# A four-layer graph network on one Trainium2 core: the first pass multiplies the adjacency by h itself, turned, and the weights are applied to its result

## The chip, the core and the metric

The kernel runs on one core of a Trainium2 chip. The core has an engine for matrix products (TensorE; PE in the rows, its weight loads are PEld), VectorE (DVE), ScalarE (ACT), GpSimd (POOL), and a queue (SP) whose only work here is to issue transfers. Each engine runs its own instructions in order and waits on semaphores for the others. The metric is the device time of one execution in microseconds (us); lower is better.

## What is computed

Node features x are 4096 x 256, the adjacency adj is 4096 x 4096. Four layers follow each other, each on h = relu(layernorm(x)). This change touches the first layer only:

```
    def _L0_gnn_ref(X, A, W):
        A2 = A + jnp.eye(A.shape[0], dtype=A.dtype)
        dscale = jnp.diagonal(A2) ** (-0.5)
        temp = A2 @ X @ W.T
        A_norm = dscale[:, None] * A2 * dscale[None, :]
        return jax.nn.relu(A_norm @ temp)
...
    h = jnp.maximum(_layernorm(x, axis=-1), 0.0)
    x = x + _L0_gnn_ref(h, adj, L0_gnn_W)
```

The first layer has two products with the adjacency: `A2 @ (h W^T)`, and then `A_norm @ temp`. The other layers are attention (layer 1), a normalised adjacency (layer 2) and two adjacency products (layer 3).

## The kernel before, in words

The adjacency is read in 8 row groups `g` of 512 rows, and each of these in 8 chunks `c` of 512 columns: 64 chunks of 1 MB per pass. There are six passes `p`: 0 and 1 are the two products of the first layer, 2 is attention, 3 to 5 are the later layers. A step numbered `PRE` ahead of pass 0 makes the moving operand of pass 0.

Every float32 operand of a product is split into two float16 parts, hi and lo, and a product is three matmuls: hi by hi, hi by lo, lo by hi. The hi part of a chunk is made by ScalarE (line L1257 in `split`), the lo part by VectorE (L1650). In pass 0 the split chunk lies in one of 4 `sets`; ScalarE may begin chunk n when TensorE is through with chunk n-4 and the stores of chunk n-4 (its halves, written back to memory for later passes) have landed. From group 1 on VectorE makes two more sums of every chunk (L1657, L1659).

The order on each engine is written out by hand. In `PRE`, for each group q of 512 rows of x: VectorE takes the statistics (`norm_stats`, L1850 to L1858), GpSimd raises the variance to the power -0.5 (L872) and makes the shift (L875), ScalarE writes relu's hi part (L1408), VectorE normalises (L1865) and writes the lo part (L1882), TensorE turns h (L1013), ScalarE copies it (L1417), TensorE multiplies it by the weight (`small`, L1076 to L1078, 24 matmuls) and ScalarE and VectorE split the result (L1445, L1906) into `mov[0]`, which is `right` in the rows. The chunks of group 0 run between these: chunk c needs the rows of x of group c alone. Ahead of them TensorE runs 60 and 60 small matmuls on the identity (`keep_warm`, L1202).

In pass 0 and in attention a block of the adjacency is stationary and 258, 256 and 258 columns of `mov` move past it (L931 to L933): 48 matmuls for a chunk. One of the 258 is a column of ones, which gives the sums of the adjacency's rows. In pass 1 (`CROSS`) the hi block meets hi and lo of `mov[1]` in one matmul of 512 columns (L928), the lo block meets hi in 256 (L929): 32 matmuls for a chunk, and VectorE adds the two halves of the result (`add_cross`, L1742). After each group its tail runs among the chunks of the next: ScalarE takes the accumulators out of PSUM (L1356 in pass 0) behind the split of chunk 0, and so on (`PLACES`).

Of the kernel before, what the change touches and what calls it, by code (L numbers as in the profile page):

```python
# [41 lines left out]
F = 256  # L42
# [20 lines left out]
WARM = [60, 60]  # L63
# [16 lines left out]
def build(nc, x, adj_t, w0, wg, bias_g, w2, bias_2, w3a, w3b, sent, sums, ready, x_mid, directs, out):  # L80
# [4 lines left out]
    with ctx:  # L85
# [6 lines left out]
        def sem(name):  # L92
# [24 lines left out]
        wraw = [shared[:, wofs[i]:wofs[i + 1]].rearrange("p (f n) -> p f n", f=FB) for i in range(5)]  # L117
# [3 lines left out]
        weights_of = {PRE: wpart[0], 1: wpart[1], 2: wpart[2], 3: wpart[3], 4: wpart[4]}  # L121
# [28 lines left out]
        hsp2 = ev[:, :, :].rearrange("p b n -> p (b n)")[:, 0:GB * F].bitcast(f16)\  # L150
            .rearrange("p (b s n) -> p b s n", s=2, b=GB)
# [23 lines left out]
        ident32 = sb("ident32", [P, P], f32)  # L175
        diag = sb("diag", [P, NB], f32)
        d = sb("d", [P, NB], f32)
        dinv = sb("dinv", [P, NB], f32)
# [27 lines left out]
        w0_loaded = sem("w0_loaded")  # L206
# [11 lines left out]
        ones_ready = sem("ones_ready")  # L218
        w_hi = sem("w_hi")
# [86 lines left out]
        SMALL = [PRE, 1, 2, 3, 4]  # L306
        SELF = [0, 1]
# [12 lines left out]
        CROSS = [1]  # L320
        PLAIN = [0, 1]

        def chunk_no(p, g, c):
            return (g + NG * PLAIN.index(p)) * NC + c

# [24 lines left out]
        def whole_of(p, c, k, b):  # L350

            first = k * GR + b * P if p == ATT else block_at(k, b)
            if p == 1 and k >= GB // 2:
                first -= 2 * QUAD
                return halved[c % 4][:, first:first + P], halved[c % 4][:, 2 * QUAD + first:2 * QUAD + first + P]
            hi, lo = sets[c % 4] if p == 0 else sets[c % 2]
            return hi[:, first:first + P], lo[:, first:first + P]

        def used_no(p, g, c):

            return chunk_no(p, g, c) - NC

        def raw_free(eng, p, g, c):

            if p == 0 and isinstance(g, int) and g == 0:
                eng.wait_ge(split_ready, c + 1)
# [7 lines left out]
        def turned_at(p, g):  # L374

            return 2 * NG if p == ATT else 2 * NG + 2 + 2 * g
# [92 lines left out]
        def work(p, g):  # L469

            return (o2, hsp2, 1) if p == PRE and g % 2 else (o, hsp, 0)

        def small_bank(p, b):
# [3 lines left out]
            if p == PRE:  # L477
                bank = (psW[:, :], psS[:, 1, :])[b // 2]
            elif p == 3:
# [11 lines left out]
        def _(sp):  # L491
# [4 lines left out]
            def load(g, c):  # L496
                if not (isinstance(g, int) and g == 0 and c < 4):

                    h, e = (g, c - 4) if c >= 4 else (g - 1, c + 4)
                    raw_free(sp, 0, h, e)  # L500
                row = g * (NC * P) + c * P
                sp.dma_start(ring[c % 4], adj_t[bass.ds(row, P), :]).then_inc(adj_loaded[c % 4], 16)

            def store_whole(g, c):

                rows = ready[bass.ds(g * (NC * P) + c * P, P), :]
                raw_free(sp, 0, g, c)
                hi, lo = sets[c % 4]
                sp.dma_start(rows[:, 0:2 * QUAD], hi[:, 2 * QUAD:4 * QUAD]).then_inc(halves_stored[c % 4], 16)
                sp.dma_start(rows[:, 2 * QUAD:4 * QUAD], lo[:, 2 * QUAD:4 * QUAD]).then_inc(halves_stored[c % 4], 16)  # L510
# [13 lines left out]
            def load_halves(g, c):  # L524

                if isinstance(g, int) and g == 0:
                    sp.wait_ge(halves_stored[c % 4], 32 * (c // 4 + 1))
# [114 lines left out]
            def load_others():  # L642
                for src, dst in zip([wg, w2, w3a, w3b], wraw[1:]):
                    sp.dma_start(dst, src).then_inc(w_loaded, 16)
                with nc.allow_non_contiguous_dma(reason="the diagonal's elements lie apart"):

                    row = GB * GR
                    for r in range(GB):
                        src = bass.AP(adj_t.tensor, block_at(r, r), [[row + 1, P], [(NC + 1) * P * row, NG]])
                        sp.dma_start(diag[:, :].rearrange("p (q r) -> p q r", r=GB)[:, :, r], src)\  # L650
                            .then_inc(diag_loaded, 16)
# [22 lines left out]

            def group_0(g):
                for c in range(2 if isinstance(g, int) and g == 0 else 0, NC):
                    load(g, c)
                    if isinstance(g, int) and g == 0 and c < 4:
                        if c == 3:
                            load_others()  # L680
                        continue
# [76 lines left out]
            sp.wait_ge(x_loaded[0], 16)  # L758
            load_x(1)
            load(0, 0)  # L760
            load_x(2)
            load_x(3)
            load(0, 1)
            for q in range(4, NG):
                load_x(q)
# [33 lines left out]
            for p in range(6):  # L799
# [22 lines left out]
                elif p == 0:  # L822
                    group_0(0)
                    group_0(1)
                    with sp.Fori(2, NG) as g:
                        group_0(g)
# [32 lines left out]
        def _(pool):  # L859
# [18 lines left out]
            def tail(p, g):  # L878
                if p in SELF:
# [3 lines left out]
                    if not (isinstance(g, int) and p == 0):  # L883
# [6 lines left out]
                if p == 0:  # L890
                    pool.wait_ge(row_ready, at([0], p, g, 2, 2))
# [16 lines left out]
            for p in [0, 1, 2, 3]:  # L908
                if p == 0:
                    tail(0, 0)  # L910
                    with pool.Fori(1, NG) as g:
                        tail(p, g)
                else:
                    with pool.Fori(0, NG) as g:
                        tail(p, g)
# [3 lines left out]
        def _(pe):  # L919
            def product(p, g, c, b, k, first, last):  # L920
# [5 lines left out]
                if p in CROSS:  # L926
# [1284 lines left out]
```

## Time and profile before

| | |
|---|---|
| median of 3 runs | 2350.82 us (2348.93 to 2351.11) |
| the profiled execution | 2350.55 us |
| its span, first to last instruction | 2348.8 us |
| before and behind the span | 1.75 us |
| PE busy | 2308.0 us (98%) |
| DVE, ACT, POOL busy | 73%, 48%, 6% |
| mean granted TensorE clock | 0.998 |

The span is the time from the first to the last instruction of the core. Busy is the time in which an engine executes; a matmul's end is modelled, so TensorE's pace is read from the distance between the starts of matmuls. The idle time before an instruction is put down to what released it.

### The profile page before, as it was taken

How to read it: one execution, taken by the hardware profiler on the slowest of the kernel's cores; microseconds unless marked ns; L12 is line 12 of the kernel's file. 1: busy time of each engine (PE TensorE's matmuls, PEld its weight loads, DVE VectorE, ACT ScalarE, POOL GpSimd, SP SyncE). 2: the span in 40 equal slices, each digit the busy share in tenths (PEclk: the TensorE clock that was granted, in tenths of full speed). 3: DMA queues.
4: the chain of work that ended last, by engine and by line, in shares of the span. 5: the costliest groups of instructions: out<-in, count | busy, mean ns of one | idle time of the engine just before them, and what ended most of it. 6: DMA issues, size and time to landing. Idle time of an engine off the chain costs nothing. (4 is left out here: it accounts for less than half of the span.)

```text
span 2348.8 us, 62852 instructions
## 1 busy us (share of the span) xinstructions
PE 2308.0 (98%) x24536; PEld 1936.3 (82%) x24536; DVE 1718.9 (73%) x2765; ACT 1131.4 (48%) x1821; POOL 140.4 (6%) x114
## 2 busy tenths in 40 slices
PE   7999999999999999999999999999999999999999
PEld 6888887666666677777778799999988888899998
DVE  7877867677777777678878967676776766667665
ACT  6634443445544555555545545545554444433332
POOL 2211101101100000000000000000000000000000
PEclk9999999999999999999999999999999999999999
DMA  8699998889887988989999999899898898999997
GB/s 287 223 361 335 355 361 298 254 263 283 274 262 226 263 282 281 280 259 308 320 294 314 298 354 328 302 340 334 302 335 328 316 350 309 329 348 382 373 378 290
DMA packets 291738, 726.86 MB, mean 309 GB/s; under 512 B 76704, under 2 KB 109728, under 8 KB 258848
## 3 DMA queue, kind: packets, MB, share of 16 engines
q1 hardware_dynamic: 291328, 724.42, 89.2%
q8 instruction: 79, 1.29, 0.2%
q10 hardware_dynamic: 288, 0.79, 0.1%
q14 instruction: 43, 0.35, 0.0%
HBM read 574.64 MB, written 138.41 MB: 304 GB/s over the span
## 5 line engine op out<-in xcount | busy, mean ns | idle before, releaser
L931 PE MATMUL acc<-right,ahi 128*128 128x258 f16 x1536 | 419.8, 273 | 4.9 <-DVE o L1742 2.1
L933 PE MATMUL acc<-right,alo 128*128 128x258 f16 x1536 | 419.3, 273 | 0.0
L932 PE MATMUL acc<-right,ahi 128*128 128x256 f16 x1536 | 418.7, 273 | 0.0
L953 PE MATMUL acc<-left,ahi 128*128 128x128 f16 x1536 | 272.0, 220 | 3.7 <-DVE alo L1726 3.7
L957 PE MATMUL acc<-left,alo 128*128 128x128 f16 x1536 | 272.1, 220 | 0.0
L956 PE MATMUL acc<-left,ahi 128*128 128x128 f16 x1536 | 272.0, 220 | 0.0
L1580 ACT ACTIVATE ahi<-en 128x512 f16<-128x512 f32 x256 | 160.3, 626 | 91.2 <-DVE en L2066 88.3
L931 PEld LDWEIGHTS acc<-right,ahi 128*128 128x128 f16 x1536 | 150.2, 98 | 41.2 <-DVE alo L2081 9.8
L928 PE MATMUL acc<-left,ahi 128*128 128x512 f16 x512 | 180.2, 379 | 0.0
L928 PE MATMUL acc<-left,en 128*128 128x512 f16 x512 | 180.2, 379 | 0.0
L953 PE MATMUL acc<-left,adj 128*128 128x128 f16 x1024 | 179.0, 220 | 0.0
L956 PE MATMUL acc<-left,adj 128*128 128x128 f16 x1024 | 178.9, 220 | 0.0
L957 PE MATMUL acc<-left,adj 128*128 128x128 f16 x1024 | 178.9, 220 | 0.0
L957 PE MATMUL acc<-left,en 128*128 128x128 f16 x1024 | 178.1, 219 | 0.0
L953 PE MATMUL acc<-left,en 128*128 128x128 f16 x1024 | 178.1, 219 | 0.0
L956 PE MATMUL acc<-left,en 128*128 128x128 f16 x1024 | 178.1, 219 | 0.0
L2081 DVE SCALAR_TENSOR_TENSOR alo<-en,ahi 128x512 f16<-128x512 f32 x256 | 175.4, 685 | 2.3 <-ACT ahi L1580 2.1
L932 PEld LDWEIGHTS acc<-right,ahi 128*128 128x128 f16 x1536 | 150.3, 98 | 29.9
L933 PEld LDWEIGHTS acc<-right,alo 128*128 128x128 f16 x1536 | 150.3, 98 | 18.7
L953 PEld LDWEIGHTS acc<-left,ahi 128*128 128x128 f16 x1536 | 150.8, 98 | 4.1 <-DVE alo L1726 4.0
L957 PEld LDWEIGHTS acc<-left,alo 128*128 128x128 f16 x1536 | 150.9, 98 | 0.0
L956 PEld LDWEIGHTS acc<-left,ahi 128*128 128x128 f16 x1536 | 150.8, 98 | 0.0
(255 smaller groups left out, 6546.1 us busy)
## 6 DMA issues: line engine op xcount, KB each, us to landing
adj<-in_adj_t SPq DMA_DIRECT2D x192, 512.0 KB, 6.1
adj<-ready SPq DMA_DIRECT2D x96, 1024.0 KB, 7.7
en<-ready SPq DMA_DIRECT2D x96, 1024.0 KB, 7.7
adj<-in_adj_t SPq DMA_DIRECT2D x32, 1024.0 KB, 8.3
en<-in_adj_t SPq DMA_DIRECT2D x32, 1024.0 KB, 8.8
en<-ready SPq DMA_DIRECT2D x64, 512.0 KB, 5.4
en<-sent SPq DMA_DIRECT2D x46, 512.0 KB, 6.9
sent<-en SPq DMA_DIRECT2D x90, 256.0 KB, 4.3
```

What stands on the lines that cost most here:

```text
L928: nc.tensor.matmul(acc[:, b, :].rearrange("p (s n) -> p s n", s=2), hi, both, start=first, stop=False)
L931: nc.tensor.matmul(acc[:, b, 0:n], hi, m[:, jb, 0:n], start=first, stop=False)
L932: nc.tensor.matmul(acc[:, b, 0:F], hi, m[:, jb, LO:LO + F], start=False, stop=False)
L933: return nc.tensor.matmul(acc[:, b, 0:n], lo, m[:, jb, 0:n], start=False, stop=last)
L953: nc.tensor.matmul(to, hi[:, rows], bhi[:, cols], start=first and i % 2 == 0 and b == 0 and k == 0, stop=False, skip_group_check=True)
L956: nc.tensor.matmul(to, hi[:, rows], blo[:, cols], start=False, stop=False, skip_group_check=True)
L957: last = nc.tensor.matmul(to, lo[:, rows], bhi[:, cols], start=False, stop=False, skip_group_check=True)
L1580: nc.scalar.activation(ahi[:, (j // GB) % 2, j % GB * GR:(j % GB + 1) * GR], nums[:, n % NUMS, :], ACT.Copy, scale=P_SCALE).then_inc(num_h ...
L2081: nc.vector.scalar_tensor_tensor(alo[:, (j // GB) % 2, cols], nums[:, n % NUMS, :], P_SCALE, ahi[:, (j // GB) % 2, cols], ALU.mult, ALU.su ...
```

## The change

- `PRE` no longer turns h nor multiplies it by the weight: `first_rows` (ScalarE, L1471 and L1474 of the new file) writes relu's hi part straight to `mov[0]`, and for every group but the first the normalised rows in float32 too, which VectorE wrote before; `lo_of_first_rows` (VectorE) writes the lo part.
- In pass 0 (`first_pass`) a 128 x 128 block of h is stationary and 512 rows of the adjacency move past it: 24 matmuls of 512 columns for a chunk. The result is (A h) turned, in two of the four banks of `acc`; the other two serve the next group. The identity of A2 is added by 16 matmuls for a group (`own_rows`).
- Groups 0 and 1 run in turn (`PAIRED`): chunks (0,0), (1,0), (0,1), (1,1), ... Chunk n of this order is number n. Chunks of group 1 carry VectorE's two sums.
- The tail of a group of pass 0 is two steps: `z` splits the turned result out of PSUM at chunk 0 of the next group, and `t`, at chunk 3, splits what `small` (24 matmuls, behind chunk 2) makes of it with the weight.
- Pass 1 takes the form of pass 0 before: 258, 256 and 258 columns, 48 matmuls for a chunk. The row sums and their power move there, `add_cross` goes.
- 40 matmuls of `keep_warm` instead of 60 and 60. The first chunk is loaded and split in two halves, and the SP queue starts without waiting for x. Weights, biases and the diagonal are loaded between the chunks of the pairs.

```diff
+PAIRED = 2
+            if p == 0 and isinstance(g, int) and g < PAIRED:
+                return PAIRED * c + g
...
+            def turned_block(g, n, c, k, f):
+                hi, lo = moving_of(n, k)
+                rows = mov[0][:, GB * c + k, :]
+                bhi, blo = rows[:, f * P:(f + 1) * P], rows[:, LO + f * P:LO + (f + 1) * P]
+                to = acc[:, 2 * (g % 2) + f, :]
+                nc.tensor.matmul(to, bhi, hi, start=c == 0 and k == 0, stop=False, skip_group_check=True)
+                nc.tensor.matmul(to, bhi, lo, start=False, stop=False, skip_group_check=True)
+                return nc.tensor.matmul(to, blo, hi, start=False, stop=False, skip_group_check=True)
...
+            def first_pass():
+                for n in range(NG * NC):
+                    g, c = place_of(n)
...
+                        pe.wait_ge(split_ready, n + 1)
+                    if g == 0:
+                        pe.wait_ge(mov_ready, at(MOVE, PRE, c, GB, 1 if c == 0 else GB))
+                    if c == NC - 1:
...
+                        own_rows(g)
...
+                    if g >= PAIRED and c == 2:
...
+                        step("W0W1", 0, g - 1 if g > PAIRED else 0)
...
-                if p in CROSS:
-                    both = m[:, jb, :].rearrange("p (s n) -> p s n", s=2)[:, :, 0:F]
-                    nc.tensor.matmul(acc[:, b, :].rearrange("p (s n) -> p s n", s=2), hi, both, start=first, stop=False)
-                    return nc.tensor.matmul(acc[:, b, 0:F], lo, m[:, jb, 0:F], start=False, stop=last)
...
+            def hi_of_z(g, side):
...
+                for f in range(FB):
+                    act.wait_ge(acc_ready, at(ALL, 0, g, GB, 2 * f + 2))
+                    nc.scalar.activation(hTq[:, f, :, :], acc[:, 2 * side + f, :].rearrange("p (b n) -> p b n", n=P),
+                                         ACT.Copy, scale=1.0 / ADJ_SCALE).then_inc(h_hi, GB // FB)
+            def hi_of_t(g):
...
+                for r in range(2):
+                    act.wait_ge(small_ready, at(SMALL, 0, g, 2, r + 1))
+                    for b in (2 * r, 2 * r + 1):
+                        nc.scalar.activation(mov[1][:, blocks(g, b), 0:F], small_out(0, b), ACT.Copy,
+                                             scale=d_w[:, blocks(g, b)]).then_inc(mov_hi, 1)
+            def first_rows(g):
+                act.wait_ge(shift_ready, at(NORM, PRE, g))
...
+                for b in range(GB):
+                    args = dict(bias=shift[:, u, b:b + 1], scale=rstd[:, u, b:b + 1])
+                    nc.scalar.activation(mov[0][:, blocks(g, b), 0:F], xres[:, GB * g + b, :], ACT.Relu, **args)\
+                        .then_inc(mov_hi, 1)
+                    if g > 0:
+                        nc.scalar.activation(normed_of(g)[:, b, :], xres[:, GB * g + b, :], ACT.Identity, **args)\
+                            .then_inc(normed, 1)
...
             split(0, 0, 0)
+            first_rows(0)
             for q in range(NG):
-                keep_hT(q, 0)
-                keep_hT(q, 1)
-                stage("W0", PRE, q)
+                if q > 0:
+                    split(0, 0, q)
+                if q + 1 < NG and q > 0:
+                    first_rows(q + 1)
+                split(0, 1, q)
                 if q == 0:
...
+                    first_rows(1)
...
+            stage("stats", PRE, 0)
+            split_first(0, first_split, first_hi)
+            stage("norm", PRE, 0)
+            lo_of_first_rows(0)
+            split_first(1, split_ready, split_hi)
             stage("stats", PRE, 1)
-            split(0, 0, 0)
             for q in range(NG):
+                if q > 0:
+                    split(0, 0, q)
+                    if q + 1 < NG:
+                        lo_of_first_rows(q + 1)
+                split(0, 1, q)
                 if q == 0:
...
+                    lo_of_first_rows(1)
                 if q + 2 < NG:
                     stage("stats", PRE, q + 2)
```

How this moves instructions is shown at two places. The first is VectorE at the start of the program, one turn of the loop over q. Before, a turn holds one chunk's lo part (L1650), the statistics of group q+2 (L1850 to L1858), and the normalised rows, their lo part and the two halves of the weight's product (L1865, L1882, L1906):

```order
L1850 BN_STATS stats<-left 128x6 x4
L1855 BN_AGGR mv<-stats 128x2 x4
L1857 TENSOR_SCALAR nmean<-mv 128x4
L1858 TENSOR_SCALAR vare<-mv 128x4
L1650 SCALAR_TENSOR_TENSOR right<-en,right 128x2048
L1865 TENSOR_SCALAR en<-left,mv,rstd 128x256 x4
L1906 SCALAR_TENSOR_TENSOR right<-psW,right 128x256 x2
L1882 SCALAR_TENSOR_TENSOR ev<-en,ev 128x4x256
L1906 SCALAR_TENSOR_TENSOR right<-psS,right 128x256 x2
```

Now the same turn reads (L2007 to L2015 are the statistics, L1770 a chunk's lo part, L1896 the lo part of h's rows, L1777 and L1779 the two sums):

```order
L2007 BN_STATS stats<-left 128x6 x4
L2012 BN_AGGR mv<-stats 128x2 x4
L2014 TENSOR_SCALAR nmean<-mv 128x4
L2015 TENSOR_SCALAR vare<-mv 128x4
L1770 SCALAR_TENSOR_TENSOR alo<-adj,ahi 128x2048
L1896 SCALAR_TENSOR_TENSOR right<-en,right 128x4x256
L1770 SCALAR_TENSOR_TENSOR alo<-adj,ahi 128x2048
L1777 TENSOR_TENSOR right<-adj 128x512
L1779 TENSOR_TENSOR right<-right,adj 128x512
```

A second chunk's lo part and its two sums have come in, between the lo part of h's rows and the next statistics; normalising and the weight's product have gone.

The second place is ScalarE in the same turn. Before, it copies the turned h (L1417), takes out the weight's product (L1445), writes relu's four hi parts (L1408) and splits one chunk (L1257):

```order
L1417 ACTIVATE hT<-psT 128x1024
L1417 ACTIVATE hT<-psS 128x1024
L1445 ACTIVATE right<-psW 128x256 x2
L1408 ACTIVATE hsp<-left,shift,rstd 128x256 x4
L1445 ACTIVATE right<-psS 128x256 x2
L1257 ACTIVATE right<-en 128x2048
```

Now it splits a chunk of group 0 (L1345), writes four hi parts (L1471) and four normalised blocks (L1474), and splits the chunk of group 1:

```order
L1345 ACTIVATE right<-en 128x2048
L1471 ACTIVATE right<-left,shift,rstd 128x256
L1474 ACTIVATE o<-left,shift,rstd 128x256
L1471 ACTIVATE right<-left,shift,rstd 128x256
L1474 ACTIVATE o<-left,shift,rstd 128x256
L1471 ACTIVATE right<-left,shift,rstd 128x256
L1474 ACTIVATE o<-left,shift,rstd 128x256
L1471 ACTIVATE right<-left,shift,rstd 128x256
L1474 ACTIVATE o<-left,shift,rstd 128x256
L1345 ACTIVATE right<-en 128x2048
```

The split of the group 1 chunk has come to stand behind eight activations, where it was one chunk a turn behind four.

## Rows read from the trace of the kernel before

**Rows 1.** Page, busy time of each engine and share of the span

```profile
PE 2308.0 (98%) x24536; PEld 1936.3 (82%) x24536; DVE 1718.9 (73%) x2765; ACT 1131.4 (48%) x1821; POOL 140.4 (6%) x114
```

**Rows 2.** Windows: busy of PE, PEld, DVE, ACT, POOL; PEclk, DMA share, GB/s

```profile
21.90:94.00 72.10, 67.00 (x654) 58.99 (x651) 57.57 (x127) 50.08 (x77) 20.21 (x13) 1.00 0.70 218
94.00:390.20 296.20, 294.88 (x2688) 262.74 (x2686) 231.46 (x232) 125.78 (x112) 42.34 (x16) 1.00 0.96 346
390.20:741.40 351.20, 351.20 (x2219) 216.88 (x2217) 250.55 (x444) 166.81 (x328) 43.55 (x37) 1.00 0.84 262
```

**Rows 3.** Waits of PE, 0 to 95 us (total, times, longest)

```profile
PE acc L1202 <- DVE vare L1858: 6.8, 1, 6.8
PE psT L1013 <- DVE ev L1882: 3.7, 4, 1.4
```

**Rows 4.** Timeline of DVE, the start and 20 to 27 us

```profile
4.41 1.41 DVE L1850 BATCH_NORM_STATS2 stats<-left 128x6 f32<-128x256 f32 x4 [3.26 <-DMA left<-in_x]
...
19.73 1.23 DVE L1882 SCALAR_TENSOR_TENSOR ev<-en,ev 128x1024 f16<-128x1024 f32 x1 [0.32 <-ACT ev L1408]
20.87 1.40 DVE L1850 BATCH_NORM_STATS2 stats<-left 128x6 f32<-128x256 f32 x4
...
22.98 2.28 DVE L1650 SCALAR_TENSOR_TENSOR alo<-adj,ahi 128x2048 f16<-128x2048 f32 x1
26.16 1.38 DVE L1865 TENSOR_SCALAR o<-left,mv,rstd 128x256 f32<-128x256 f32 x4 [0.90 <-POOL rstd L872]
```

**Rows 5.** Timeline of POOL, 20 to 35 us

```profile
23.15 2.98 POOL L872 TENSOR_TENSOR rstd<-vare,neghalf 128x4 f32<-128x4 f32 x1 [5.64 <-DVE vare L1858]
...
32.71 1.01 POOL L872 TENSOR_TENSOR rstd<-vare,neghalf 128x4 f32<-128x4 f32 x1 [6.30 <-DVE vare L1858]
```

**Rows 6.** Timeline of ACT, 26 to 29 us

```profile
26.44 2.08 ACT L1408 ACTIVATE hsp<-left,shift,rstd 128x256 f16<-128x256 f32 x4 [1.04 <-POOL shift L875]
28.42 0.63 ACT L1445 ACTIVATE right<-psS 128x256 f16<-128x256 f32 x2
```

**Rows 7.** Timeline of ACT at two group boundaries

```profile
179.84 0.39 ACT L1356 ACTIVATE ev<-acc 128x257 f32<-128x257 f32 x1 [0.93 <-PE acc L933]
180.13 1.90 ACT L1257 ACTIVATE ahi<-adj 128x2048 f16<-128x2048 f32 x1
...
221.98 0.39 ACT L1356 ACTIVATE ev<-acc 128x257 f32<-128x257 f32 x1 [0.93 <-PE acc L933]
```

**Rows 8.** Timeline of DVE behind the first of these boundaries

```profile
182.06 2.29 DVE L1650 SCALAR_TENSOR_TENSOR alo<-adj,ahi 128x2048 f16<-128x2048 f32 x1 [8.93 <-ACT ahi L1257]
...
185.60 1.22 DVE L1807 TENSOR_TENSOR o<-ev,own 128x1024 f32<-128x1024 f32 x1
```

**Rows 9.** Timeline of PE: `small` and behind it, then the end of pass 1

```profile
13.84 0.28 PE L1076 MATMUL psW<-wsp,hT 128*128 128x256 f16 x1 [0.67 <-ACT hT L1417]
...
16.47 3.51 PE L1202 MATMUL acc<-ident 128*128 128x128 f16 x60
...
741.45 0.38 PE L1171 MATMUL psS<-right 128*128 128x512 f16 x1
...
741.88 0.38 PE L1173 MATMUL psS<-right 128*128 128x512 f16 x1
```

**Rows 10.** Waits of PE, 700 us to the end

```profile
PE acc L953 <- DVE alo L1726: 3.7, 1, 3.7
PE acc L931 <- DVE o L1742: 2.1, 1, 2.1
```

**Rows 11.** Windows behind the first of these waits, and early

```profile
1352.00:1354.00 2.00, 2.00 (x20) 2.00 (x21) 0.00 (x0) 0.00 (x0) 0.00 (x0) 0.50 0.97 405
1356.00:1360.00 4.00, 4.00 (x59) 4.00 (x57) 0.00 (x0) 0.26 (x1) 0.00 (x0) 0.76 1.00 412
...
6.00:24.00 18.00, 15.06 (x196) 14.09 (x197) 14.73 (x43) 13.55 (x19) 5.26 (x5) 1.00 1.01 412
```

**Rows 12.** Groups of ACT in pass 1, 440 to 740 us

```profile
L1405 ACT ACTIVATE o<-left,shift,rstd 128x256 f32 x28 | 14.4, 586 | 0.0
```

More of the change, by code:

```diff
@@ L62 @@
 OWN = 5
-WARM = [60, 60]
+WARM = 40
+PAIRED = 2
 LEAD = 3
@@ L467, in sent_rows, with normed_of @@
             return 2 * P * (sum(NC - 1 - h for h in range(g)) + c - g - 1)
-        def work(p, g):
-            return (o2, hsp2, 1) if p == PRE and g % 2 else (o, hsp, 0)
+        def normed_of(g):
+            return (o, o2)[g % 2]
         def small_bank(p, b):
@@ new lines, in own_rows @@
+            def own_rows(g):
+                for f in range(FB):
+                    for b in range(GB):
+                        rows = mov[0][:, GB * g + b, :]
+                        to = acc[:, 2 * (g % 2) + f, b * P:(b + 1) * P]
+                        nc.tensor.matmul(to, rows[:, f * P:(f + 1) * P], scaled_ident[:, :], start=False, stop=False,
+                                         skip_group_check=True)
+                        nc.tensor.matmul(to, rows[:, LO + f * P:LO + (f + 1) * P], scaled_ident[:, :], start=False, stop=False,
+                                         skip_group_check=True)
@@ L1207, in _ @@
             pe.wait_ge(var_ready, 2)
-            keep_warm(WARM[0])
-            pe.wait_ge(w_ready, 1)
-            pe.wait_ge(ones_ready, 1)
-            for s in ["T0T1", "W0", "W1"]:
-                step(s, PRE, 0)
-            keep_warm(WARM[1])
-            step("T0T1", PRE, 1)
+            keep_warm(WARM)
             for p in range(6):
@@ L1256, in split @@
                             act.wait_ge(chunk_done, at(PLAIN, p, g, NC - 1, c - 3 if c >= 4 else c - 2))
-                    nc.scalar.activation(sets[c % 4][0], ring[c % 4], ACT.Copy, scale=ADJ_SCALE).then_inc(split_hi, 1)
+                    if first and c == 0:
+                        act.wait_ge(first_loaded, 16)
+                        for i, made in enumerate((first_hi, split_hi)):
+                            part = slice(i * 2 * QUAD, (i + 1) * 2 * QUAD)
+                            nc.scalar.activation(sets[0][0][:, part], ring[0][:, part], ACT.Copy, scale=ADJ_SCALE).then_inc(made, 1)
+                        return
+                    nc.scalar.activation(sets[n % 4][0], ring[n % 4], ACT.Copy, scale=ADJ_SCALE).then_inc(split_hi, 1)
                     return
+                act.wait_ge(adj_loaded[c % 4], at(PLAIN, p, g, 16 * NC // 4, (c // 4 + 1) * 16))
                 if c >= 2:
@@ L1847, in norm_stats @@
                 dve.sem_inc(passed, 1)
-                u = work(p, g)[2]
+                u = g % 2 if p == PRE else 0
                 for b in range(GB):
@@ L1954, in stage @@
             def stage(name, p, g):
-                if name == "ev" and p in CROSS:
-                    for b in range(GB):
-                        add_cross(p, g, b)
-                elif name == "ev" and p in STR:
+                if name == "ev" and p in STR:
                     mix(p, g)
@@ L2109, in lo_of_weights @@
                 dve.wait_ge(w_hi, n)
[L2110 removed]
+                nc.vector.scalar_tensor_tensor(wsp[:, 1, part], wplain[:, part], W_SCALE, wsp[:, 0, part],
                                                ALU.mult, ALU.subtract).then_inc(w_ready, 1)
[L2114 to L2116 removed]
+            dve.wait_ge(const_ready, 3)
```

471 lines of the change are left out of this document (275 added, 196 removed).

## The prediction, made before the changed kernel ran

> **What bounds the kernel now.** I read the page first: TensorE is busy for 98% of the span and VectorE for 73% [rows 1], so what TensorE does not stream or wait for is worth nothing here. Then windows by stage [rows 2]: in groups 1 to 7 of pass 0 TensorE is busy for 294.9 of 296.2 us, in pass 1 for all 351.2 us. In the stretch with `PRE` and group 0 it is busy for 67.0 of 72.1 us. The waits of the start [rows 3] show where it stands: 6.8 us for the first statistics, and 3.7 us in four waits for h's lo part. So the start is the one place where TensorE already hangs on a chain of the other engines, and the rest is its own stream.
>
> The transfers are near their limit in pass 0 (346 GB/s at a share of 0.96), but 412 GB/s were moved early on [rows 11].
>
> **The change, part by part.**
>
> *Paces.* In pass 0 a group takes 221.98 - 179.84 = 42.1 us [rows 7], or 5.27 us for a chunk of 48 matmuls, 0.110 us each. `small` runs from 13.84 to 16.47: 2.63 us for 24 [rows 9]. A matmul of 512 columns starts 0.215 us behind the last: 741.45 to 741.88 for two [rows 9]. A chunk of 24 of those is 5.17 us. Columns streamed are nearly the same (512 x 24 against 772 x 16), so the new form by itself saves 0.1 us per chunk and no more.
>
> *The rest of pass 0, groups 2 to 7.* 48 chunks x 5.17 = 248.4 us. `own_rows` is 16 matmuls of 128 columns for a group; 60 took 3.51 us [rows 9], so 0.9 us, 5.4 in six groups. `small` stands here seven times: 18.4 us. Sum 272.2 us.
>
> The tails could add to it. `z` needs the group's last matmul. The 257 columns of L1356 take 0.39 us and the next split starts 0.29 us behind their start [rows 7]; two of 512 columns are some 1.2 us, of which half lies under the last matmuls. The split then takes 1.93 us until VectorE starts (180.13 to 182.06) and VectorE 2.29 [rows 7, 8]: 4.9 to 5.0 us behind the group's end, and TensorE wants that chunk at 5.2. `t` waits for `small` behind chunk 2; after it ScalarE has two products' halves, a split, and VectorE a lo part: about 5.1 us behind the end of `small` (0.1 + 0.9 + 1.9 + 2.2), against 5.2 of work. Both just fit; I put 0.1 us for a boundary, 0.7 us in all. If they miss, it is 0.5 us a time, 6 us.
>
> *The start.* This is where the sum is decided. Groups 0 and 1 run in turn, so a group of h's rows feeds two chunks, 10.35 us of work for TensorE. But the engines run in written order, and the order makes a loop: VectorE's statistics of group q+2; GpSimd's power and shift; ScalarE's eight activations of that group; ScalarE's split of chunk (1, q+1), which stands behind them; VectorE's lo part of it and its two sums; then the statistics of q+3. Nothing in that loop overlaps with itself:
> - From the statistics' start to the first activation: 26.44 - 20.87 = 5.57 us [rows 4, 6]. In this the power takes 2.98 us though it takes 1.01 when VectorE stands still [rows 5]: VectorE runs the next chunk's lo part (22.98, 2.28 us) [rows 4], and the power ends 0.87 us behind it. In the new order the same instruction stands behind the statistics, so the same 5.57.
> - Eight activations: four take 28.42 - 26.44 = 1.98 us [rows 6]; 3.96.
> - The split up to VectorE's start: 1.93 [rows 7, 8].
> - The lo part and the two sums: 185.60 - 182.06 = 3.54 [rows 8].
>
> Sum 15.0 us for a pair against 10.35 us of matmuls: TensorE stands for 4.65 us in every pair. Before, a turn held one chunk, turning and `small`; eight of them took 72.1 us with TensorE busy for 67.0 [rows 2], so 9.0 us for 8.4 of work: the waits were small because the loop was short.
>
> Now the clock time. x's first rows land at 4.41 [rows 4]; now 1 MB of the adjacency shares the way, at 412 GB/s up to 2.5 us, and I take 0.8: 5.2. Statistics 2.1, then half a lo part (1.2) and the power's 0.9: 9.5, ScalarE at 9.8. VectorE: normalising 1.38 [rows 4], four lo parts of 0.42, half a lo part 1.2: the statistics of group 1 start near 13.8. TensorE starts at 11.4, where `small` started at 13.8 and pass 0 at 21.9. 13.8 + 5.57 + 3.96 + 1.23 (lo part of the rows, as L1882 [rows 4]) = 24.6: statistics of group 2. Five turns of 15.0 later, at 99.6, those of group 7. From there 5.57 + 3.96 + 1.93 + 2.25 = 13.7: chunk 13 is ready at 113.3. Three chunks (15.5) and two `own_rows` (1.8): 130.6 us, where 16 chunks without a wait would be done at 11.4 + 82.8 + 1.8 = 96.0.
>
> Pass 0 then ends at 130.6 + 272.2 + 0.7 = 403.5, before at 390.2 [rows 2]: **+13.3 us**.
>
> *Pass 1.* Before 351.2 us [rows 2], with seven `small`. Now eight groups of 42.1 us, 337.0, and eight `small`, 21.0: 358.0. **+6.8 us**. The 512 columns go to the place where they were already 512, two in three, and it loses them. GpSimd gets a power of about 3 us more a group there; its users come chunks later, so nothing. `add_cross` goes from VectorE, which has slack; only at the start of attention did TensorE wait for it, 2.1 us [rows 10]: **-2.1 us**.
>
> *The clock.* After the wait of 3.7 us [rows 10] the granted clock was 0.50 of full, 1.2 GHz, in 1352 to 1354 and 0.76 on the mean in 1356 to 1360 [rows 11]; with 0.50 between them too, 2 + 1 = 3.0 us are lost. The new waits of 4.65 us are longer. A fall inside a pair is free, since 10.35 + 3.0 is under 15.0 (it even shortens the next wait, so that falls may come in every other pair). Only the one ahead of chunk 13 counts, when TensorE becomes the bound: 0 or 3.0, I take **+1.5 us**. The Trainium skill speaks against this change here: "TensorE: Matmul & The Clock Gate", section "Loop structure matters more than you think", counts a wait between bursts of matmuls twice, since the array then runs at half its clock. By the rule the fall comes behind every such wait and the last costs 3.0 (total 2371.5), by the trace of one case it may; the 1.5 above stands either way.
>
> The 80 matmuls of `keep_warm` that go lay in waits. The SP queue has a load or store each 2.5 us at most, and a pair moves 3.9 MB in 15 us, 262 GB/s against the 412 shown [rows 11]: hidden, unless the pair shrank to 9.5.
>
> **Sum.** 2350.55 (the profiled execution; 0.3 under the median of the runs) + 13.3 + 6.8 - 2.1 + 1.5 = 2370.05; **2370 us**, 0.8% slower.
>
> **The rivals.**
>
> *The loop is as I read it, with nothing worse* (0.70): 2370; its own range is 2363 to 2378, from the clock (0 or 3), x's landing (0.8 less, 1.5 more) and the tails.
>
> *The power is not held up* (0.08). If VectorE's lo part comes a little later than the power, the power takes 1.01 [rows 5] and a turn 13.0. Seven turns or parts of them x 2.0 = -13.8: 2356. Against it: the two start within 0.2 us of each other in the trace [rows 4, 5], and the written order is the same.
>
> *The activations are slower* (0.11). In pass 1 the same instruction to float32 takes 0.586 us [rows 12], 0.09 more: x 8 x 7 = +5.1. With both falls of the clock paid and the tails missing, 2370 + 5.1 + 1.5 + 5 = 2381.
>
> *The start keeps up with TensorE, and the kernel is faster* (0.11). This decides as soon as a pair's loop is under 10.35 us, which would need 4.65 us of the loop to lie beside each other: the split of the group 1 chunk ahead of the activations, or statistics two turns ahead. Then group pair 0 ends at 96.0 and the clock stays: 2370.05 - 34.6 - 1.5 = 2334. For it: everything but the order has room, VectorE has 9.1 us of work in a pair and ScalarE 7.8. Against it: the order as printed, in which I find no way round.
>
> That the 512 columns are faster than their count is a part of no case: 0.215 us is what the trace has for them.
>
> **How the numbers follow.** About 0.2% (4.7 us) is what a measurement of this kernel can tell from no change: 2346 to 2355.5. Slower holds the first and third case and half of the second, 0.85; the other half of the second is the same, with a margin for a mixture, 0.05; faster is the last, less a little, 0.10. The range leaves out the last case, and reaches from between the second and the first to the end of the third: 2354 to 2381.
>
> **What the changed profile would show.** Right: in windows from 12 to 115 us TensorE is busy for about 70%, in waits of 4 to 5 us ahead of every chunk of group 1, released by VectorE's lo part; statistics start every 15 us; the power takes 2.98 us in them; the last chunk of the pairs ends near 131, pass 0 near 403, pass 1 358 us later; and attention starts without a wait. The clock shows 1.2 GHz behind some of the waits. Wrong: statistics every 10 us, or pass 0 ending before 390; a chunk of 512 columns that takes other than 5.17 us; or waits at the group boundaries of more than 0.3 us, the tails mis-sized.

## The result, and the profile after

The changed kernel takes **2372.73 us** (median of 4 runs, 2370.89 to 2375.57) against 2349.9 beside it: ratio 1.0098, 95% interval 1.0080 to 1.0115. It is slower by 1%, 2.7 us over the 2370.0 that was forecast. The profiled execution took 2370.89 with a span of 2369.1, 20.3 over the span before.

I went through the stages first, as in [rows 2]: windows of the changed kernel (busy time of PE, PEld, DVE, ACT and POOL, each with its count, then PEclk, DMA share and GB/s).

```profile
0.00:12.40 12.40, 3.93 (x41) 3.86 (x42) 5.62 (x19) 4.91 (x7) 3.40 (x11) 1.00 0.86 330
12.40:134.40 122.00, 97.64 (x422) 41.45 (x423) 75.47 (x121) 63.79 (x79) 27.92 (x15) 0.90 0.84 281
134.40:406.50 272.10, 272.10 (x1413) 133.35 (x1411) 189.03 (x184) 103.72 (x88) 0.31 (x1) 1.00 0.91 321
406.50:764.60 358.10, 358.10 (x3266) 319.37 (x3265) 241.65 (x441) 167.16 (x329) 50.66 (x43) 1.00 0.85 258
764.60:1372.40 607.80, 591.54 (x4625) 453.99 (x4623) 482.09 (x899) 331.26 (x626) 15.08 (x19) 1.00 0.90 288
```

Pass 0 ends at 406.4 in place of 390.2 (+16.2), pass 1 takes 358.1 in place of 351.2 (+6.9), attention 607.8 in place of 610.6 (-2.8), the rest is the same. From 134.4 on pass 0 has no idle time on TensorE. What is lost lies in the second window, where TensorE is busy for 97.6 of 122.0 us, and that at a mean clock of 0.90.

The waits of PE from 0 to 420 us, which answer to [rows 3] (total, times, longest):

```profile
PE acc L1062 <- DVE alo L1770: 14.0, 7, 4.0
PE acc L1062 <- DVE right L1770: 10.4, 4, 5.7
PE acc L1283 <- DVE vare L2015: 8.5, 1, 8.5
```

`alo` and `right` are two names of the ring's low halves. Both rows are one kind of wait: for VectorE's low part of a chunk, 24.4 us in eleven waits. DVE's timeline over one turn says why it is late (start, duration, in brackets the idle time before):

```profile
40.51 1.40 DVE L2007 BATCH_NORM_STATS2 stats<-left 128x6 f32<-128x256 f32 x4
...
42.62 2.28 DVE L1770 SCALAR_TENSOR_TENSOR alo<-adj,ahi 128x2048 f16<-128x2048 f32 x1
50.22 1.22 DVE L1896 SCALAR_TENSOR_TENSOR right<-en,right 128x1024 f16<-128x1024 f32 x1 [5.32 <-ACT en L1474]
51.95 2.29 DVE L1770 SCALAR_TENSOR_TENSOR alo<-adj,ahi 128x2048 f16<-128x2048 f32 x1 [0.51 <-ACT ahi L1345]
54.16 0.68 DVE L1777 TENSOR_TENSOR right<-adj 128x512 f32<-128x512 f32 x1
54.88 0.69 DVE L1779 TENSOR_TENSOR right<-right,adj 128x512 f32<-128x512 f32 x1
55.49 0.74 DVE L2007 BATCH_NORM_STATS2 stats<-left 128x6 f32<-128x256 f32 x2
```

The period is 55.49 - 40.51 = 14.98 us, and the last statistics start at 100.42, five periods behind 25.52. VectorE itself stands idle for 5.3 us of each: it waits for the activations that its own statistics set off. In between lies GpSimd, and behind it ScalarE (two views, POOL's and ACT's timeline):

```profile
42.78 2.98 POOL L929 TENSOR_TENSOR rstd<-vare,neghalf 128x4 f32<-128x4 f32 x1 [11.72 <-DVE vare L2015]
45.85 0.20 POOL L932 TENSOR_TENSOR shift<-nmean,rstd 128x4 f32<-128x4 f32 x1
```

```profile
46.08 0.60 ACT L1471 ACTIVATE right<-left,shift,rstd 128x256 f16<-128x256 f32 x1 [7.34 <-POOL shift L932]
...
50.03 1.89 ACT L1345 ACTIVATE ahi<-adj 128x2048 f16<-128x2048 f32 x1
```

### The profile page after: what moved, and what is told of

The parts are those of the page before. It is cut to its first block and busy times, and to the rows that moved or that the text cites. A ratio compares the mean times of both kernels' runs of the same rounds, so it can differ in the third digit from the quotient of the medians.

```text
span 2369.1 us, 61174 instructions
## 1 busy us (share of the span) xinstructions
PE 2314.1 (98%) x23944; PEld 1884.2 (80%) x23944; DVE 1674.6 (71%) x2687; ACT 1114.6 (47%) x1786; POOL 112.0 (5%) x107
## 5 line engine op out<-in xcount | busy, mean ns | idle before, releaser
L982 PE MATMUL acc<-right,ahi 128*128 128x258 f16 x1024 | 280.5, 274 | 1.7 <-DVE alo L2245 1.4
L984 PE MATMUL acc<-right,alo 128*128 128x258 f16 x1024 | 280.1, 274 | 0.0
L983 PE MATMUL acc<-right,ahi 128*128 128x256 f16 x1024 | 279.7, 273 | 0.0
L1699 ACT ACTIVATE ahi<-en 128x512 f16<-128x512 f32 x256 | 160.2, 626 | 89.8 <-DVE en L2230 85.4
L1396 ACT ACTIVATE ahi<-en 128x512 f16<-128x512 f32 x191 | 118.5, 620 | 53.4 <-DVE en L1833 53.4
L982 PE MATMUL acc<-left,ahi 128*128 128x258 f16 x512 | 139.8, 273 | 0.0
L984 PE MATMUL acc<-left,alo 128*128 128x258 f16 x512 | 139.8, 273 | 0.0
L982 PE MATMUL acc<-left,en 128*128 128x258 f16 x512 | 139.8, 273 | 0.0
L984 PE MATMUL acc<-left,en 128*128 128x258 f16 x512 | 139.8, 273 | 0.0
```

Of the source, the lines that this page charges most:

```text
L982: nc.tensor.matmul(acc[:, b, 0:n], hi, m[:, jb, 0:n], start=first, stop=False)
L983: nc.tensor.matmul(acc[:, b, 0:F], hi, m[:, jb, LO:LO + F], start=False, stop=False)
L984: return nc.tensor.matmul(acc[:, b, 0:n], lo, m[:, jb, 0:n], start=False, stop=last)
L1396: nc.scalar.activation(ahi[:, c % 2, 2 * QUAD:3 * QUAD], s1_of(p, g, c), ACT.Copy, scale=ADJ_SCALE)\
L1699: nc.scalar.activation(ahi[:, (j // GB) % 2, j % GB * GR:(j % GB + 1) * GR], nums[:, n % NUMS, :], ACT.Copy, scale=P_SCALE).then_inc(num_h ...
```

## The experiments

Ten runs stand in this section, the last of them the changed kernel again; times are medians, and each ratio is to the kernel before, run beside it. `q` counts the turns of the start.

### The order on VectorE: statistics ahead of the low parts

```diff
                     split(0, 0, q)
+                    if q + 2 < NG:
+                        stage("stats", PRE, q + 2)
                     if q + 1 < NG:
                         lo_of_first_rows(q + 1)
                 split(0, 1, q)
                 if q == 0:
+                    stage("stats", PRE, 2)
                     lo_of_first_rows(1)
-                if q + 2 < NG:
-                    stage("stats", PRE, q + 2)
```

> The changed kernel with one instruction group moved on VectorE: the statistics of group q+2 stand ahead of the lo part of h's rows in turn q (in turn 0 too), not behind the second chunk's sums. Nothing is added or left out. Theory of the loop (statistics, power, eight activations, split of the group 1 chunk, lo part, sums, statistics again: 15.0 us a pair): the loop now spans two turns, 17.3 us for two pairs, so TensorE sets the pace with 10.35 us. Statistics then start every 10.3 to 10.6 us, the pairs end near 102 us instead of 134, and the kernel takes 2341 us (2337 to 2346), less than the kernel before. Rival, the transfers set the pace of the pairs (3.9 MB for a pair): the period cannot fall much below 12 us, pairs end near 115, total 2354. Rival, the clock or the form of the matmuls is what costs: period stays at 15, total 2372.

**2344.95 us** (2343.14 to 2347.73), ratio 0.9973 [0.9964, 0.9983], in the range expected. Nothing is taken out, two lines stand elsewhere, and the kernel is 27.8 us faster than the changed one and 6.1 us faster than the kernel before, run beside it. From turn 1 on the statistics start at 28.47, 37.73, 46.71, 58.49, 68.17. Of the eleven waits two are left:

```profile
PE acc L1062 <- DVE right L1770: 4.2, 1, 4.2
PE acc L1062 <- DVE alo L1770: 1.0, 1, 1.0
```

Pass 0 ends at 377.8 in place of 406.4. So the loop of the written order is the cause of the start's loss; the work in it is not. The transfers are not either: behind the wait of 4.2 us TensorE has no further wait in the pairs.

### The order on ScalarE and VectorE: the split ahead of the activations

```diff
@@ ScalarE
+                split(0, 1, q)
                 if q + 1 < NG and q > 0:
                     first_rows(q + 1)
-                split(0, 1, q)
@@ VectorE
-                    if q + 1 < NG:
-                        lo_of_first_rows(q + 1)
                 split(0, 1, q)
+                if q > 0 and q + 1 < NG:
+                    lo_of_first_rows(q + 1)
```

> The changed kernel with the split of chunk (1, q) ahead of the eight activations on ScalarE and its lo part and sums ahead of the lo part of h's rows on VectorE; the statistics stay at the end of the turn. Nothing is left out. Theory of the loop: split, lo part and sums fall out of it, and the lo part of the rows comes in: 5.57 + 3.96 + 1.2 = 10.7 us a pair, 0.4 above TensorE's 10.35. Statistics start every 10.7 to 10.8 us, pairs end near 103 to 105, total 2342 (2338 to 2348). Rival, only the place of the statistics matters (VectorE is the bound, not the round through ScalarE): period 15, total 2372. Rival, transfers: total 2354.

**2353.75 us** (2351.12 to 2356.83), ratio 1.0008 [0.9999, 1.0017]: most of the loss is gone, but I missed by 12 us. The period is 11.97 in place of 10.7. DVE's timeline and POOL's show the missing 1.3:

```profile
49.53 1.40 DVE L2007 BATCH_NORM_STATS2 stats<-left 128x6 f32<-128x256 f32 x4
...
51.63 4.49 DVE L1770 SCALAR_TENSOR_TENSOR right<-en,right 128x2048 f16<-128x2048 f32 x2
```

```profile
51.81 2.98 POOL L929 TENSOR_TENSOR rstd<-vare,neghalf 128x4 f32<-128x4 f32 x1 [7.59 <-DVE vare L2015]
54.86 1.32 POOL L932 TENSOR_TENSOR shift<-nmean,rstd 128x4 f32<-128x4 f32 x1
```

Two low parts now run end to end (x2, 4.49 us), and the *second* GpSimd instruction is held as well: the shift takes 1.32 in place of 0.20 and ends at 56.18, 0.06 behind the second low part. The first activation starts 56.21 - 49.53 = 6.68 us behind the statistics, not 5.57. I had carried the 5.57 over unchanged into an order in which something else stands behind the statistics.

### What holds the power: the sums, or the low part?

Two experiments on the 2.98 us. In the first the two sums of the group 1 chunk move out of `split` (which leaves them out where `late` is set) into `two_sums`, behind the next statistics, so that the first of them, and not the low part, is what VectorE does when the power starts:

```diff
-                split(0, 1, q)
+                split(0, 1, q, late=0 < q < NG - 2)
                 if q + 2 < NG:
                     stage("stats", PRE, q + 2)
+                if 0 < q < NG - 2:
+                    two_sums(0, 1, q)
```

> The changed kernel with the two sums of the group 1 chunk (1.35 us) behind the statistics instead of ahead of them, for the five turns of the loop. They leave the loop as written, but VectorE then runs them, and the next lo part behind them, while GpSimd's power waits. Theory, GpSimd's power ends 0.87 us behind the end of VectorE's run of two-input instructions whatever its length: the power takes 4.3 us instead of 2.98, and the period stays at 15.0 (14.9 to 15.1), total 2372. Rival, the power takes a fixed 2.98 us or is held by the lo part alone: period 13.6, total 2372 - 6.7 = 2366.

**2366.55 us** (2364.12 to 2367.52), ratio 1.0062 [1.0047, 1.0078], period 13.89. The theory, that the power waits for the end of VectorE's whole run of two-input instructions, fell. The rival's time (2366) came out, but neither of its two reasons: the power took neither a fixed 2.98 us, nor was it held by the low part alone. POOL's timeline:

```profile
41.51 1.38 POOL L929 TENSOR_TENSOR rstd<-vare,neghalf 128x4 f32<-128x4 f32 x1 [10.40 <-DVE vare L2020]
42.97 2.04 POOL L932 TENSOR_TENSOR shift<-nmean,rstd 128x4 f32<-128x4 f32 x1
```

The first sum ran from 41.34 to 42.03 and the power ended 0.86 behind its end, as it ended 0.86 behind the low part's end (44.90) in the changed kernel. The shift that followed was then held by the low part (42.67 to 44.96) and ended at 45.01. Power and shift together took 3.50 us in place of 3.27, which is most of why the period is 13.89 and not 13.6. So GpSimd can get in between two instructions of VectorE. A gap between them isn't needed: in `split_first` the power ended at 54.79, while two low parts ran end to end from 51.63 to 56.12.

In the second one VectorE simply waits until GpSimd is done, before the low part of the group 0 chunk:

```diff
                 if q > 0:
+                    if q + 1 < NG:
+                        dve.wait_ge(shift_ready, at(NORM, PRE, q + 1))
                     split(0, 0, q)
```

> The changed kernel with one wait more: in turns 1 to 6 VectorE's low part of the group 0 chunk (2.28 us) waits until GpSimd's shift of the same turn is ready, so GpSimd's power runs with no two-input instruction beside it. Theory (the power's 2.98 us are 1.01 held up by that low part): power 1.0, shift 0.2, first activation 3.6 us behind the start of the statistics in place of 5.57, the low part moved into VectorE's idle 5.3 us; period of the pairs 15.0 - 1.9 = 13.1, pass 0 ends some 9 to 10 earlier, time 2363 (2361 to 2365). Rival one (the power takes 2.98 whatever VectorE does, as it did behind the one-input statistics): the low part comes 3.2 later, the period stays 15.0 and the time 2373. Rival two (the delayed low part takes the place of the wait: it is late for TensorE's chunk and pushes the first rows' low parts): period 14 to 15, time 2368 to 2374.

**2359.38 us** (2357.59 to 2360.46), ratio 1.0037 [1.0024, 1.0051]. A wait was added and 13.4 us came back, more than the 2361 to 2365 expected allow. POOL and DVE:

```profile
40.94 1.01 POOL L929 TENSOR_TENSOR rstd<-vare,neghalf 128x4 f32<-128x4 f32 x1 [11.72 <-DVE vare L2015]
42.03 0.20 POOL L932 TENSOR_TENSOR shift<-nmean,rstd 128x4 f32<-128x4 f32 x1
```

```profile
42.27 2.29 DVE L1770 SCALAR_TENSOR_TENSOR alo<-adj,ahi 128x2048 f16<-128x2048 f32 x1 [1.40 <-POOL shift L932]
```

The power takes 1.01, the period is 13.02 (38.66 to 51.68), and chunk 13 starts at 102.54 in place of 114.21: five periods shorter by 1.96 and the same gain once more in the last turn, 11.7. I had counted five (9 to 10 us) and forgotten the last. Pass 0 ends 13.1 us earlier (393.3 for 406.4); the rest of that is the clock's: ahead of chunk 13 TensorE now waits for 0.5 us, and the clock is at 1.00 behind it, where the changed kernel's chunk took 1.65 us longer in its first profile. The prediction's rival with a power that is not held up had a turn of 13.0; its time was 2356.

The Trainium skill, "SBUF — State Buffer", section "SBUF: two separate sides", calls it a lock: an instruction of VectorE with two SBUF inputs and one of GpSimd exclude each other, and who starts first has the ports until its end. The 2.98, 1.38 and 1.01 us agree with that; the 5.22 us of `stats1_first`, below, span the ends of several such instructions and aren't explained by it.

### The clock: matmuls without use in the waits

```diff
+                    if n < PAIRED * NC - 2 and (n % 2 == 1 or n == 2) and n > 1:
+                        for _ in range(50):
+                            nc.tensor.matmul(psS[:, 1, 0:P], ident[:, :], ident[:, :], start=True, stop=True)
                     if n == 0:
                         pe.wait_ge(first_split, 1)
```

> The changed kernel with 50 matmuls of 128 columns on the identity (2.8 us) ahead of chunk 2 and of the odd chunks 3 to 13, where TensorE waits 4 to 6 us. They write a bank that is not in use. Theory, a fall of the clock inside a pair is free because the loop sets the pace and only the one ahead of chunk 13 counts: the falls in the pairs go (mean granted clock of 12 to 131 us from 0.90 to about 1.00), statistics start every 15.0 us as before, and the total falls by 1.6 us, 2371. Rival, every fall costs 3.4 us: total 2372.7 - 4 x 3.4 = 2359.

**2373.4 us** (2372.0 to 2376.81), ratio 1.0093 [1.0078, 1.0109]: no gain, and the 2371 expected was missed. Both kernels in the window of the pairs, the changed one first and then this one:

```profile
12.00:131.00 119.00, 94.64 (x414) 40.17 (x411) 72.62 (x119) 62.68 (x79) 27.92 (x15) 0.90 0.84 284
```

```profile
12.00:131.00 119.00, 106.15 (x771) 58.37 (x769) 72.62 (x120) 63.54 (x80) 27.91 (x15) 1.00 0.83 283
```

The mean clock rises from 0.90 to 1.00, and the period of the statistics stays 14.98. A low clock inside a pair only uses up the next wait: in the changed kernel's profile chunks 2, 5 and 9 took 2.8, 2.6 and 3.0 us longer than 5.17, and without these falls the period is the same. The rival in which every fall costs (2359) is refuted. Pass 0 ends 1.1 us earlier (405.3 for 406.4), since the chunk 13 of this profile ran at full clock; but so it did in the second profile of the changed kernel, at the end of this section. And attention takes 611.1 in this profile, 3.3 more than in the changed kernel's first, so the total is no shorter.

### Pass 1's form alone

The kernel before with `CROSS` empty: pass 0 is untouched, pass 1 runs as in the changed kernel, in moving tiles of 258, 256 and 258 columns.

```diff
-        CROSS = [1]
+        CROSS = []
...
-                    nc.vector.tensor_tensor(o[:, :, :], ev[:, :, 0:F] if p == 0 else o[:, :, :], own[:, :, :], ALU.add)\
+                    nc.vector.tensor_tensor(o[:, :, :], ev[:, :, 0:F], own[:, :, :], ALU.add)\
...
-                elif p == ATT:
-                    ev_used(0, NG - 1)
+                elif p in (1, ATT):
+                    ev_used(p - 1, NG - 1)
```

> The kernel before with the second half of the change undone in pass 1 alone, or rather done there alone: pass 0 stays as before, pass 1 runs in the form that the changed kernel gives it (moving tiles of 258, 256 and 258 columns into one accumulator, and the recentring of the accumulator waits as in the other passes). Theory: pass 1 costs what it cost between the profiles before and after, +6.8 (358.1 against 351.2), and the attention behind it starts at the better point, -2.1 to -2.5: time 2350.8 + 4.5 = 2355.3 (2354 to 2357). Rival (those 6.8 us are the stores and sums of pass 0's new form reaching into pass 1, not pass 1's own instructions): no change, 2350 to 2351.

**2351.1 us** (11 runs, 2347.8 to 2355.71), ratio 1.0002 [0.9993, 1.0011]. The expected 2355.3 lies outside. Its windows of pass 1 and attention:

```profile
389.80:745.20 355.40, 355.40 (x3243) 317.02 (x3241) 239.68 (x416) 166.83 (x328) 43.53 (x37) 1.00 0.84 259
745.20:1351.90 606.70, 590.94 (x4627) 452.67 (x4624) 482.08 (x895) 331.20 (x626) 14.03 (x18) 1.00 0.90 289
```

Pass 1 takes 355.4: +4.2 for the form. I had written +6.8 into the expectation; 2.6 of it is an eighth `small`. The changed kernel applies pass 0's weights to the result, so that of pass 0's last group falls into pass 1: in PE's groups each of the six `small` rows counts x32 there, and x28 here. In this kernel all eight of pass 0 stand at its start. And attention takes 606.7 in place of 610.6: the wait of 2.1 us for `o` [rows 10] is gone, and the other waits on VectorE in it (`psS <- DVE en`) are 7.6 us in place of 10.9. The two together leave next to nothing. That is one profile each: two profiles of the changed kernel differ by 1.5 us in attention (607.8 and 609.3), so of the 3.9 us only the 2.1 have a cause that the rows show.

### How far it goes

Three versions on top of `stats_earlier`. In the first the statistics of group 1 also stand ahead of the normalising of group 0 at the very start, and ScalarE's activations of group 1 wait until that is done (both count on `normed`).

```diff
             split_first(0, first_split, first_hi)
+            stage("stats", PRE, 1)
             stage("norm", PRE, 0)
             lo_of_first_rows(0)
             split_first(1, split_ready, split_hi)
-            stage("stats", PRE, 1)
```

> The version with each statistics ahead of the low parts (measured 2344.95), and besides the statistics of group 1 moved ahead of VectorE's normalising of group 0, at the very start. Theory: the one long wait left in pairs, 4.2 us ahead of chunk 2, is the activations of group 1 that begin 5.8 us behind statistics at 14.57; with statistics at 8.5 those activations begin near 14.5, chunk 0 starts 2.0 later (normalising of group 0 is pushed by 2.1), so of the 4.2 us some 4 go and 2 come: 2343 (2341 to 2345). Rival (chunk 2 waits for its own adjacency split, not for the rows): 4.2 stays, 2.0 come: 2347.

**2342.14 us** (2340.79 to 2343.04), ratio 0.9965 [0.9951, 0.9978], in the range expected. The wait ahead of chunk 2 is 2.6 in place of 4.2. It did not go completely, and one row of POOL's timeline says why:

```profile
13.31 5.22 POOL L932 TENSOR_TENSOR shift<-nmean,rstd 128x4 f32<-128x4 f32 x1
```

An instruction of 0.20 us took 5.22, up to 18.53; in VectorE's run of two-input instructions from 13.11 to 19.20 one ended at 18.48 and the next started at 18.51. The second version lets VectorE wait for it once:

```diff
             lo_of_first_rows(0)
+            dve.wait_ge(shift_ready, 2)
             split_first(1, split_ready, split_hi)
```

> The version stats1_first (measured 2342.14) with one wait more: before the low part of chunk 0's second half VectorE waits until GpSimd's shift of group 1 is there. In stats1_first that shift, a multiplication of 128x4 that takes 0.20 when VectorE is idle, started at 13.31 and took 5.22, until VectorE's run of two-input instructions (13.11 to 19.1) ended. Theory (GpSimd gets nothing while VectorE runs two-input instructions end to end, and a pause of 0.2 on VectorE lets it finish): shift ready near 14.7 in place of 18.5, activations of group 1 begin at 14.9 in place of 18.56, the low part of chunk 2 is ready near 25 in place of 26.7, the wait ahead of chunk 2 shrinks from 2.6 to about 0.8, and the time is 2340.4 (2339.5 to 2341.5). Rival (the shift is held for another reason, the semaphore from the power or the order on GpSimd): it still takes over 4 us, VectorE now stands for it, everything behind comes 4 later: 2345 to 2347.

The same instruction, and PE's waits behind it:

```profile
13.33 1.28 POOL L932 TENSOR_TENSOR shift<-nmean,rstd 128x4 f32<-128x4 f32 x1
```

```profile
24.91 0.39 PE L1062 MATMUL acc<-right 128*128 128x512 f16 x1 [0.69 <-DVE right L1772]
33.16 0.61 PE L1062 MATMUL acc<-right 128*128 128x512 f16 x1 [2.90 <-DVE right L1772]
```

**2343.82 us** (2340.72 to 2346.07), ratio 0.9966 [0.9954, 0.9978]. The mechanism is as the theory had it: the shift is ready at 14.6, the activations start at 14.78, and the wait ahead of chunk 2 is 0.7. The time is not: a wait of 2.9 us has come up ahead of chunk 3, and against `stats1_first` no difference can be measured.

The third lets SyncE hold its first adjacency DMA back until the rows of x are there:

```diff
                 if n == 0:
+                    sp.wait_ge(x_loaded[0], 16)
```

> The version with each statistics ahead of the low parts (measured 2344.95), and SyncE issues its first adjacency DMA only when the rows of x of group 0 have landed. Theory (the x rows land 1.7 us later than in the kernel before because two adjacency DMAs issued at 0.74 share the queues with them): statistics at 4.5 in place of 6.27, but the first adjacency half now lands near 9, its split and low part end near 12.5: chunk 0 starts 0 to 1 later than now; time 2345 to 2346.5. Rival (chunk 0 depends on the x rows alone): chunk 0 starts 1.7 earlier, time 2343.3.

**2345.03 us** (2342.42 to 2347.72), ratio 0.9977 [0.9968, 0.9986]: no change, as expected. The statistics start at 4.25 in place of 6.27, and chunk 0 at 13.19 in place of 12.69, since the adjacency is later.

### The changed kernel again

> The changed kernel once more beside the others, as a check on the size of each verdict: 2372.7 (2370 to 2375), ratio 1.0098 again. Rival (its clock falls in the pairs differ from run to run and are part of its loss): 2368 or lower.

**2372.92 us** (2371.86 to 2374.55), ratio 1.0095 [1.0079, 1.0110]. The time and the period (14.98) are the same again, the falls of the clock are not. PE's timeline, the start of three chunks behind waits; 0.38 us is a matmul of 512 columns at full clock, 0.6 one at half:

```profile
54.48 0.39 PE L1062 MATMUL acc<-ahi,right 128*128 128x512 f16 x1 [3.99 <-DVE alo L1770]
69.46 0.61 PE L1062 MATMUL acc<-right 128*128 128x512 f16 x1 [2.76 <-DVE right L1770]
114.41 0.39 PE L1062 MATMUL acc<-ahi,right 128*128 128x512 f16 x1 [2.77 <-DVE alo L1770]
```

Behind the first of these waits the clock fell only from the fourth matmul on, behind the second at once, and behind the third, ahead of chunk 13, not at all. Pass 0 ended at 405.3 and not 406.4, and the profiled execution still took 2371.86, 1.0 more than the first. The mean clock from 12 to 131 us was 0.93 here. The rival's first half holds (the falls differ from run to run), its second doesn't: the time isn't 2368 or lower.

## Why the prediction was right

**The loop of a pair, 15.0 us.** Measured 14.98, with the power at 2.98 in each of its turns. `stats_earlier` shows that the written order makes the loop, `hold_free` that the hold is 1.96 us of it. The rival in which the start keeps up was refuted for the kernel as written, and its condition, "statistics two turns ahead", is what `stats_earlier` fulfils: it gave 2344.95, where the rival had 2334. Of these 11 us a later start (12.7 for 11.4), the waits of 4.2 and 1.0 us and a fall of the clock behind the longer one (1.7) explain 8.2.

**The clock times.** x landed later than I took it (statistics at 6.12, not 5.2), chunk 13 started at 114.21 for 113.3. TensorE was done with the pairs at 133.2 for 130.6: 0.9 from that, 1.65 from the clock, for which the sum had +1.5 in another term.

**Groups 2 to 7, 272.2 + 0.7.** 273.2 measured from 133.2 to 406.4, with no wait at a boundary. The tails fit, so the 0.7 put down for waits there was needed for none; where the 1.0 us over the 272.2 lies, the rows don't say.

**Pass 1, +6.8.** Measured +6.9. `pass1_form` splits it into +4.2 for the form and 2.6 for the `small` that changed its stage.

**Attention, -2.1.** The wait for `o` is gone, and attention is 2.8 us shorter in this profile. The size isn't shown by that: in the second profile of the changed kernel attention takes 609.3, and in `hold_free`, `stats_earlier` and `stats1_first`, where the wait is gone too, attention takes 610.4, 610.1 and 609.8, and the row `psS <- DVE en` of its waits is 10.3 to 11.5 us in these four in place of 8.7. What sets these few us, from kernel to kernel and from run to run, stays open.

**The clock, +1.5.** I had 0 or 3.0 for the fall ahead of chunk 13. The fall came in the first profile and cost 1.65: the chunk took 121.03 - 114.21 = 6.82 us for 5.17, at 1.2 GHz to some 117.5. In the second profile it didn't come. So the 1.5, a mean of two cases, was near the 1.65 by luck. In the first profile the windows of 5.7 us from the start of chunks 5, 7, 9 and 11 had PEclk 0.54, 1.00, 0.50 and 1.00: a fall in every other pair, as the prediction thought possible, behind waits of 3.99 us and not behind the 1.9 and 1.5 that a slow pair leaves. The second profile doesn't repeat that: falls came behind waits of 5.74, 3.99, 2.76 and 3.99 (and for three matmuls in chunk 0, behind none), but not behind 3.08 and 2.77. `fill_waits` shows that the falls inside the pairs cost nothing. The Trainium skill, "TensorE: Matmul & The Clock Gate", section "Loop structure matters more than you think", has the matmuls behind a long wait run at the low clock. The trace agrees for four of the eleven waits of the first profile, and only the last of the four cost time.

**The signs.** TensorE was busy for 78.6 of 103 us from 12 to 115, 76% and not some 70%, since matmuls at half clock count as busy for longer. A wait of 4 us stood ahead of every other chunk of group 1, not of every one: behind a slow pair it was 1.2 to 1.9, and three waits of 0.28 stood ahead of chunks of group 0.

The sum of the terms was 2370.05 for the profiled execution, which took 2370.89, the fastest of the four. That it is met to 0.8 us is in part luck: pass 0 took 1.4 us more than its terms with the clock's, attention 0.7 less. The median lies 2.7 us above. The mechanism, the loop of 15.0 us a pair that VectorE's written order closes, is what the runs show.

## What to carry to other kernels

Two tiles of work for every set of inputs doesn't help when the set's own chain, written in one order over three engines, closes a loop longer than the work: read one period of the engine that is idle *and* waited for, and look which of its instructions starts the chain. Put that one first. Here the order of two calls was worth 27.8 us, more than the whole change cost. A tiny instruction of GpSimd on such a chain can be stretched by the two-input instruction that VectorE runs beside it (1.01 to 2.98 us here), so a wait added on VectorE can shorten the loop; and each stall removed was followed by the next one, so count the gain at the end of the stage.

## What the runs showed of the hardware

- The same GpSimd power of 128x4 took 1.01 us beside an idle VectorE (`hold_free`), 1.38 beside a two-input instruction of 128x512 (`sums_later`), 1.92 beside one of 128x1024 (`stats_earlier`) and 2.98 beside one of 128x2048 (the changed kernel). In the last three it ended some 0.86 us behind the end of that instruction.
- The shift behind it, 0.20 us alone, took 1.32 (`split_first`), 2.04 (`sums_later`) and 5.22 (`stats1_first`) where VectorE's two-input instructions followed each other. In the last case several of VectorE's instructions ended without letting it in; in `stats_earlier` the power got in at the first such end. Why is open.
- Falls of TensorE's clock to 1.2 GHz left the period of the pairs at 14.98 us, in which TensorE waits anyway, though the mean clock of 119 us fell to 0.90 (the changed kernel against `fill_waits`). Where in the pairs the falls came differed between two profiles of one kernel.
